# Seven block products in place of eight for the first feed-forward layer of two token tiles, in four of six blocks

## The reference

```python
def _block(x, w1, b1, w2, b2):
    h = jax.nn.gelu(jnp.einsum('bsd,hd->bsh', x, w1) + b1, approximate=False)
    return jnp.einsum('bsh,dh->bsd', h, w2) + b2 + x

def _layernorm(x, g, b):
    mu = jnp.mean(x, axis=-1, keepdims=True)
    var = jnp.mean(jnp.square(x - mu), axis=-1, keepdims=True)
    return (x - mu) * jax.lax.rsqrt(var + LN_EPS) * g + b

for i in range(6):                       # w1 is 1024 x 256, w2 is 256 x 1024
    x = _block(x, W1[i], B1[i], W2[i], B2[i])
    if i < 5:
        x = _layernorm(x, LN_G[i], LN_B[i])
```

## Time and profile before

| what | value |
|---|---|
| median of 3 runs | 625.2 us (624.97 to 625.22) |
| profiled execution, its span | 625.31 us, 623.5 us |
| PE busy | 617.3 us, 99% of the span |
| DVE, ACT, POOL busy | 459.9, 409.0, 248.7 us (74%, 66%, 40%) |
| share of PE in the chain of work that ended last | 95% |
| DMA | 25.13 MB, 40 GB/s over the span |

### The profile page before, as it was taken

The page is one execution under the profiler, slowest core; times in us unless marked ns, Lnnn a source line. Parts: engine busy times, 40 slices in busy tenths (PEclk is TensorE's granted clock), DMA queues, the critical chain, the costliest instruction groups (busy, mean ns, idle before and its releaser), DMA issues.

```text
span 623.5 us, 8868 instructions
## 1 busy us (share of the span) xinstructions
PE 617.3 (99%) x2893; PEld 516.5 (83%) x2893; DVE 459.9 (74%) x826; ACT 409.0 (66%) x688; POOL 248.7 (40%) x233
## 2 busy tenths in 40 slices
PE   9999999999999999999999999999999999999996
PEld 7888888888888888888888888888888888888886
DVE  6999758886677778676787667767766867666676
ACT  6999986778756675566566556755656665555554
POOL 6666501537434353334532253442344422301234
PEclk9999999999999999999999999999999999999999
DMA  7210000003111020101200110200111100003544
GB/s 293 69 35 1 2 2 0 4 1 106 36 39 40 7 68 6 37 6 37 58 20 3 39 39 2 72 6 5 37 39 38 38 4 6 5 3 68 94 91 156
DMA packets 55821, 25.13 MB, mean 40 GB/s; under 512 B 46816, under 2 KB 51808, under 8 KB 55776
## 3 DMA queue, kind: packets, MB, share of 16 engines
q1 hardware_dynamic: 53376, 24.05, 15.2%
q10 hardware_dynamic: 2400, 0.52, 0.4%
HBM read 20.03 MB, written 4.52 MB: 39 GB/s over the span
## 4 chain that ended last, share of the span: by engine, by line
PE 95%; DVE 1%; DMA 1%; POOL 1%; ACT 0%; issue 0%; ACTq 0%; SPq 0%
PE BK L166 47%; PE BK L356 40%; PE BK L306 4%; PE BK L267 1%; PE BK L270 1%; PE BK L268 1%; PE BK L240 1%; PE BK L260 0%; PE BK L252 0%; PE BK L251 0%; DMA X<-in_x 0%; PE BK L230 0%; DVE R L709 0%; DMA turns<-TB 0%; DMA R<-turns 0%; DVE ST L675 0%
## 5 line engine op out<-in xcount | busy, mean ns | idle before, releaser
L976 ACT ACTIVATE HH<-BK,SM 128x512 fp32r<-128x512 f32 x192 | 132.1, 689 | 153.3 <-PE BK L166 148.3
L569 DVE TENSOR_TENSOR HL<-BK,HH 128x512 fp32r<-128x512 f32 x192 | 131.2, 685 | 84.0 <-ACT BK L982 82.0
L166 PE MATMUL BK<-XH,WL 128*128 128x512 f32 x416 | 162.4, 390 | 0.0
L166 PE MATMUL BK<-XL,WH 128*128 128x512 f32 x416 | 162.1, 390 | 0.0
L166 PE MATMUL BK<-XH,WH 128*128 128x512 f32 x416 | 162.0, 389 | 0.0
L356 PE MATMUL BK<-HH,WL 128*128 128x512 f32 x368 | 143.5, 390 | 0.0
L356 PE MATMUL BK<-HH,WH 128*128 128x512 f32 x368 | 143.2, 389 | 0.0
L356 PE MATMUL BK<-HL,WH 128*128 128x512 f32 x368 | 143.2, 389 | 0.0
L982 ACT ACTIVATE BK<-BK,SM 128x512 f32<-128x512 f32 x192 | 125.2, 655 | 0.0
L166 PEld LDWEIGHTS BK<-XH,WL 128*128 128x128 f32 x416 | 78.1, 188 | 16.6 <-DVE MS L551 0.3
L166 PEld LDWEIGHTS BK<-XH,WH 128*128 128x128 f32 x416 | 78.1, 188 | 16.3
(11 more groups left out here) (165 smaller groups left out, 790.1 us busy)
## 6 DMA issues: line engine op xcount, KB each, us to landing
STG<-in_w SPq DMA_DIRECT2D x24, 512.0 KB, 3.8
G<-sums SPq DMA_DIRECT2D x160, 8.0 KB, 1.7
out<-R SPq DMA_DIRECT2D x16, 128.0 KB, 2.0
X<-in_x SPq DMA_DIRECT2D x3, 512.0 KB, 7.7
R<-turns SPq DMA_DIRECT2D x3, 512.0 KB, 4.1
turns<-SA SPq DMA_DIRECT2D x12, 64.0 KB, 2.0
sums<-P SPq DMA_DIRECT2D x40, 8.0 KB, 1.4
R<-in_wv SPq DMA_DIRECT2D x1, 512.0 KB, 5.4
```

Source lines behind the costliest of these rows:

```text
L166: r = eng.matmul(dst, s, m, start=i == 0, stop=i == len(todo) - 1)
L569: eng.tensor_tensor(HL[:, g % HR, :], bank["mm1", n, j][:, :], HH[:, g % HR, :].bitcast(f32), ALU.subtract).then_inc(S["hlo"], 1)
L976: eng.activation(HH[:, g % HR, :], bank["mm1", n, j][:, :], ACT.Gelu, bias=B1[:, 8 * (n // 4) + j:8 * (n // 4) + j + 1]).then_inc(S["ghi"], 1)
```

## The change

In blocks 1 to 4 (`PAIRED`) the first layers of tiles 0 and 1 are computed together by Strassen's scheme. Take the weights W1 in four parts (two halves of the hidden features, two halves of the input features) and the inputs of the two tiles in four parts (two feature halves, two tiles): the plain way needs eight products of such parts, and the scheme needs seven, with sums of weights and sums of inputs ahead of them and sums of products behind. A tile pair runs in four rounds q of 128 hidden features from each half. Each product is still three matmuls, so a round has 21 + 24 = 45 matmuls (seven products and four `mm2`) where it had 48. A block that is paired thus has 12 fewer, and the other two tiles of it run as before.

What is added in each paired block:

- POOL: four sums of weight parts, 128x512 each, straight from the staging tile (`sadd`), and four low parts of them (`slo`); once, the small table `DL` of bias differences.
- ACT: high parts of four input sums (`thi`) and of three single inputs (`bhi`) in the place of four `xhi`, two high parts of weight sums of 128x1024 (`shi`), and eight copies of a product from a bank, four to another bank (`bcopy`) and four to SBUF (`tcopy`, into KB).
- DVE: four input sums (`tsum`), seven low parts (`tlo`, `blo`) in the place of four `xlo`, and eight sums of a bank and KB into a bank (`dsum`, `esum`).

The tiles 4b and 4b + 1 now end together, since their units alternate; the second accumulator pair, the semaphores for the trips of partial sums (two for each, by parity) and the homes of the inputs in XH and XL are changed to fit. With that, the hand-written lists of DVE, ACT, POOL and SP are in a new order from the later tiles of block 0 on. The list of PE is unchanged for block 0.

```diff
+PAIRED = (1, 2, 3, 4)
...
+            def prod1(b, q, a, c, d, e):
+                claim(a)
+                pe.wait_ge(S["plo"], 7 * (b - 1) + 4)
+                pe.wait_ge(S["wp_lo"], 8 * b + 4)
...
+                product(BK[a], w_ffn(b, 128 * q, 128), home(B11), True, True).then_inc(S["prod"], 1)
...
+            for b in range(1, NB):
+                if b in PAIRED:
+                    a, e, c, d = STEADY
+                    for q in range(4):
+                        g = 32 * b + 4 * q
+                        prod1(b, q, a, c, d, e)
+                        prod5(b, q)
+                        mm2(*unit(g - 3))
+                        prod2(b, q)
+                        prod6(b, q)
+                        mm2(*unit(g - 2))
+                        prod3(b, q)
+                        prod7(b, q)
+                        mm2(*unit(g - 1))
+                        prod4(b, q)
+                        mm2(*unit(g))
+                        e, c, d = d, e, c
...
+            def dsum(b, q):
+                _, c, d, _ = bank["pair", b, q]
+                ve.wait_ge(S["prod"], 12 * (b - 1) + 3 * q + 3)
+                ve.wait_ge(S["pcopy"], 8 * (b - 1) + 2 * q + 2)
+                ve.wait_ge(*bank["before", b, q][1])
+                eng.tensor_tensor(d[:, :], c[:, :], KB[:, q % 2, :], ALU.add).then_inc(S["padd"], 1)
```

641 lines of the change are left out of this document (443 added, 198 removed).

## The result

| what | before | after |
|---|---|---|
| median | 625.21 us (624.97 to 625.23, 4 runs) | 636.31 us (635.27 to 636.89, 4 runs) |
| ratio | | 1.0177, 95% interval 1.0159 to 1.0194 |
| profiled execution, its span | 625.31, 623.5 us | 636.89, 635.1 us |

What follows compares the result with a forecast made beforehand. PE, busy 99%, was taken to bound the kernel. Stalls of 3.5 + 3.2 + 4.2 + 1.0 + 1.0 = 12.9 us less the gain of 10.9 gave +2.0 on 625.3, so 627.3 us, range 620.5 to 633.0.

Steps and rivals of the forecast that it cites:

- D: Inside the rounds: `dsum`, `esum` or `bcopy` late for the next product at 32 places; 0 to 3 us, taken as 1.0.
- E: Granted clock falling in the pauses at A and B; 0 to 5.8 us for two, taken as 1.0.
- A: End of block 0: PE waits before tile 3's transposes for the later shift and fourth `l3_nm`; 3.5 us.
- B: Start of block 1: first product waits for the fourth low part, `blo` 1; 2.8 to 4.5 us, taken as 3.2.
- C: Starts of blocks 2, 3 and 4: DVE reaches `blo` 1 late; 1.6, 1.6 and 1.0, 4.2 us in all.
- The gain: On PE, 12 matmuls fewer in each of four blocks, 48 x 0.2266 = 10.9 us, with nothing added there.
- The floor of 2.8: Start of block 1: the least PE wait from instruction order alone, `ghi`, `thi`, `bhi`, `blo` in turn; 2.8 us.
- A hit costs up to 0.3: Inside the rounds: price of one late `dsum` or `esum` when DVE is inside another instruction of 0.6 us.
- No row shows a fall inside the work: Reason given for taking only 1.0 us for clock falls, out of 0 to 5.8 for two.
- Rival 5: POOL and DVE meet at each start, the clock falls once: 18.5 us of stalls, 632.9 us, chance 0.16.
- Rivals 1 to 3: Little stall, 614.5 to 619, chance 0.07; DVE keeps up at block starts, 621.7, 0.20; no change, 624.9, 0.20.
- A and B under 2 us, or gaps under 9.6 in sum: Sign on PE's timeline that the forecast is wrong: small gaps at A and B, or small gaps in all.

Runs made afterwards that it cites:

- the edit of A: Changed kernel with tile 3's shift ahead of `rsd(0)` on POOL and its fourth `l3_nm` beside the other three on ACT: 635.95 us; with shorter POOL work too, 629.27 us.
- the powers: Changed kernel with each weight sum and its low part on POOL replaced by a power over six columns, about as long: 632.72 us, ratio 1.0115.
- second and third of the new orders: Changed kernel, complete, paired blocks' layer norms of tiles 0, 1 earlier, tile 2 later; third keeps block 1's DVE and ACT order: 656.96 and 656.54 us.
- the edit of B: Changed kernel with block 1's last input high parts, sums and low parts earlier on ACT and DVE, block 2's `sadd` waiting for four low parts: 634.13 us, ratio 1.0147.

## Why the prediction was right, and where it was wrong

Against the forecast the profile has 9.6 us more. D is 3.9 of them and E 2.4, and 3.9 are of kinds that the sum had no term for; A, B and C together came 0.6 below. So the steps that failed are the price of a hit in D and the 1.0 for E. That A, B and C came out near their sizes is in part luck, as told below.

**The gain**, 10.9: right as a count of matmuls and their pitch, 9.6 where nothing else was changed. One new wait has 0.7 of the difference; the rest is open.

**A**, 3.5, measured 3.0. The steps hold one by one. The shift began at 150.90 (forecast 150.8 to 151.4), ACT's fourth `l3_nm` ended at 156.57 (156.1 to 156.7). PE's last matmul ahead of it was 0.44 us later than in the kernel before, which is the late start. What was missing is what A covers: it was treated as a price that goes away when A is mended. It doesn't; with A mended, `sum2(1)` takes 2.7 of it back. So A's size was right and its meaning was not. This is shown by the edit of A with POOL's work at full length (0.4 gained) and short (A gone for good).

**B**, 3.2, measured 3.4. The floor of 2.8 was met to 0.05 us in three kernels with lighter POOL work. Above it stands 0.6 of contention, in rows 2.66 for two `nn` and 1.78 for a `tsum`. The floor's mechanism was right. That the size was right too is luck: the low part came near 186.6 whenever PE arrived, and where the clock did not fall after A, B was 4.98 us. The 3.4 are what A and the slow clock had left of it.

**C**, 4.2 as 1.6, 1.6, 1.0; measured 3.9 as 2.40, 1.16, 0.31. The sum was right and the shares weren't: block 2 has one meeting with POOL (1.0 us, shown by the powers), blocks 3 and 4 are better than counted. That the work on DVE is the cause is shown by its removal.

**D**, 1.0, measured 4.9: the first term that was mis-sized. The step that failed is "A hit costs up to 0.3", which took an occupied DVE to mean an instruction of 0.6 us. The long ones are another kind: DVE doesn't work but stands, 2.2 to 2.9 us, at `tot1`, for 8 KB that queue beside 512 KB pieces, and `nn` behind it is slowed beside `wp_lo`. These two waits, 0.94 and 1.62, are half of D. Of the rest, 0.83 is a `bcopy` behind two `wp_hi` that had waited for their weights (0.74 and 0.28); the others are hits of 0.18 to 0.56 us, most of them above the 0.3 that was allowed, and no run takes them apart. The rows of before had the weight pieces and the sums on one queue, and the order showed `tot1` ahead of `dsum`; I costed instructions by length and forgot those that wait. The bound of 3 was too low as well.

**E**, 1.0, measured 3.4: the second. "No row shows a fall inside the work" was true because the kernel before had no pause of PE inside the work. A forecast with two pauses of 3 us should have taken the price that its own bound gave, 2.9 each, or half of it. A fall costs 1.0 to 2.6 us in these profiles (5 to 13 matmuls 0.43 us apart), less than 2.9, since the clock comes back sooner than at the start. It isn't sure for a pause: of 42 pauses of 2.15 us or more in all profiles after the first 100 us, 29 had a fall in them or behind them, among them 2.15, 2.37, 3.04 and 4.98, and others of 2.15, 2.40, 3.07 and 3.37 had none. Two falls followed shorter pauses, of 1.98 and 2.11 us, in the second and third of the new orders. What E is worth by itself the runs don't settle: with both pauses filled only 0.7 came back, since the fall behind A was covered by B; in the kernel with the edit of B the two runs at the lower clock took 1.8 to 2.0 us more.

**Not in the sum**, 3.9: slower pitch in rounds, the matmul after each wait, 0.4 of start. These make the difference between 633.0, where five terms of right size would have led, and the 636.9 of the profiled execution. Why the pitch in a round is 0.230 I didn't test. It stands with short POOL and DVE work too, so it isn't the work that was cut there; the copies and sums of products stayed whole in every experiment, so they remain a candidate.

**The rivals.** Rival 5, which counted meetings at each start and one fall of the clock, came closest with 632.9, at 0.16. Its A, B and C were too high and its D and E too low, so it came close by errors that cancel. Rivals 1 to 3 all put D and E at 0.5 or less. The criterion "A and B under 2 us, or gaps under 9.6 in sum" was not met: both gaps are above 3, and the gaps sum to 15.

**The terms aren't independent.** My theory after the result fell: undone one by one (A, B, the clock, D), the edits gave 0.4, 2.2, 0.7 and 1.0 us, where their terms are 3.0, 3.4, 3.4 and 4.9. (The runs of one kernel differ by up to 5 us, so a gain of 1 is at the edge of what they tell.) A, B and the clock between them lie on one path, POOL's queue to `sum2(1)` to the layer norm of tile 1 to its low parts, and the end of block 0 has no slack on POOL (22.12 of 22.70 us busy). PE pays for the latest of several late things, and mending one shows the next. Shorter work on POOL (5.8 us) and on DVE (6.8 us) is what gave time back. What stays open is whether a complete order exists that is under 625.2; five tries say only that I didn't find one, and that the steps I moved had no free place.

## What to carry to other kernels

Where TensorE is busy 99% of the time, a matmul saved counts nearly in full (9.6 of 10.9 us here), and a wait of PE that the saving brings can cost as much as it is long: a scheme that trades matmuls for vector work and joins two tiles at one point must pay for the joining point, not for the busy time. In an in-order queue, cost what stands at the head and waits (for a DMA, for a sum on a slow engine) before what is long, and put whatever PE needs ahead of it. Don't add up stalls as if each could be removed: undo them one at a time in thought, and ask what is late next, and count a possible fall of the clock behind each pause of about 2 us or more.

## What the runs showed of the hardware that I had not expected

- The clock can fall after a pause of 1.98 us inside a busy stretch, and can stay up after one of 3.37 us. A fall costs 1.0 to 2.6 us. It also widens the spread of the runs: in the kernel with idle matmuls they took 634.4 and 635.0 us at a mean granted clock of 1.000, 636.3 at 0.996 and 639.5 at 0.990.
- A POOL power over 128x6 takes 1.37 us (5.49 for four) and leaves DVE at full speed; a POOL sum of 128x512 takes 1.30 alone and makes an `nn` 1.33 to 1.83 instead of 0.71, while it becomes 1.62 to 1.80 itself.
- A transfer of 8 KB took 3.9 us between two of 512 KB, against 1.4 as the median of the program.
- The second matmul after a wait starts 0.34 us behind the first, not 0.23.
